# Eight neighbouring rows of an expert's second weights in each partition, and the strided reads that go with them

## What is computed

```python
# E = 8 experts, K = 2 of them for each token, FF = 1024, all float32
router_weights = softmax(xf @ rw + rb);  topw, topi = top_k(router_weights, 2);  topw = softmax(topw)
h   = gelu(einsum('td,edf->etf', xf, w1) + b1[:, None, :], approximate=False)   # w1: (8, 256, 1024)
eo  = einsum('etf,efd->etd', h, w2) + b2[:, None, :]                            # w2: (8, 1024, 256)
out = einsum('etd,te->td', eo, combine)        # combine holds topw at the two chosen experts
```

## Time and profile before

| | us |
|---|---|
| runs shown | 766.80, 769.13, 770.72 |
| median | 769.13 |
| the profiled execution | 768.74 |
| its span (first to last recorded work) | 767.0 |
| TensorE busy in it | 717.6 (94%) |
| DVE / ACT / POOL busy | 498.9 / 370.0 / 287.2 |

### The profile page before, as it was taken

The page is one execution under the profiler, slowest core; times in us unless marked ns, Lnnn a source line. Parts: engine busy times, 40 slices in busy tenths (PEclk is TensorE's granted clock), DMA queues, the critical chain, the costliest instruction groups (busy, mean ns, idle before and its releaser), DMA issues.

```text
span 767.0 us, 14561 instructions
## 1 busy us (share of the span) xinstructions
PE 717.6 (94%) x4969; PEld 482.2 (63%) x4969; DVE 498.9 (65%) x1376; ACT 370.0 (48%) x749; POOL 287.2 (37%) x558
## 2 busy tenths in 40 slices
PE   6889999999999999999988598999999999999983
PEld 4444434535464455555553485898899999999941
DVE  4579788688766877755786443455666666666436
ACT  3325466665757677677743245424333233332403
POOL 8305522543653554535752232312223322322114
PEclk9999999999999999999996799999999999999997
DMA  8954421343253022315037742586999999999754
GB/s 263 287 142 132 116 94 45 84 126 127 51 160 124 13 59 82 91 47 136 16 109 268 238 153 79 184 284 199 332 341 328 334 336 346 335 332 345 236 179 165
DMA packets 95154, 140.29 MB, mean 183 GB/s; under 512 B 11855, under 2 KB 81077, under 8 KB 92597
## 3 DMA queue, kind: packets, MB, share of 16 engines
q1 hardware_dynamic: 76357, 107.86, 44.6%
q10 hardware_dynamic: 15072, 22.02, 8.6%
q0 software_dynamic: 3648, 9.45, 3.5%
HBM read 110.65 MB, written 28.65 MB: 182 GB/s over the span
## 4 chain that ended last, share of the span: by engine, by line
PE 74%; issue 8%; DVE 6%; DMA 6%; POOL 3%; ACT 1%; SPq 0%; DVEq 0%; ACTq 0%; POOLq 0%
PE out_acc L984 12%; PE score_pair L961 10%; PE work L932 9%; PE score_pair L855 8%; PE work L849 8%; PE work L906 6%; PE work L1008 4%; PE score_pair L849 3%; DVE neg_part_max L1469 3%; PE work L855 3%; PE work L918 2%; PE work L992 2%; DMA arena<-parts_scratch 2%; PE work L935 2%; PE out_acc L849 1%
## 5 line engine op out<-in xcount | busy, mean ns | idle before, releaser
L1469 DVE TENSOR_REDUCE neg_part_max<-work 128x1 f32<-128x512 f32 (+4 forms) x368 | 213.1, 624 | 72.5 <-PE work L935 36.0
L1244 ACT ACTIVATE arena<-score_pair 128x1024 f32<-128x1024 f32 (+2 forms) x224 | 179.0, 840 | 74.9 <-PE score_pair L961 73.6
L932 PE MATMUL work<-arena 96*128 96x77 bf16 (+4 forms) x640 | 118.9, 280 | 15.8 <-DMA arena<-parts_scratch 7.8
L961 PE MATMUL score_pair<-arena 99*128 99x512 bf16 (+2 forms) x448 | 104.5, 338 | 2.3 <-DMA arena<-negmax_scratch 1.6
L984 PE MATMUL out_acc<-arena 128*32 128x512 f32 (+4 forms) x896 | 104.6, 521 | 0.8 <-DVE arena L1489 0.8
L1901 POOL DMA_INDIRECT chosen_scratch<-arena,scatter_rows x36 | 35.5, 987 | 177.8 <-DVE arena L1401 177.5
L932 PEld LDWEIGHTS work<-arena 96*128 96x128 bf16 x640 | 50.0, 100 | 79.6 <-issue 35.9
L855 PE MATMUL score_pair<-arena 128*128 128x256 f32 x432 | 97.6, 379 | 0.0
L1957 POOL TENSOR_SCALAR_AFFINE_SELECT arena<-arena 128x256 f32<-128x256 f32 x128 | 51.7, 412 | 117.2 <-ACT arena L1244 116.1
L1177 ACT ACTIVATE arena<-work,expert_b_cols 128x128 f32<-128x128 f32 x180 | 51.2, 370 | 84.1 <-PE work L849 78.3
L849 PE MATMUL work<-arena 128*128 128x128 f32 x720 | 89.1, 282 | 0.3 <-issue 0.3
(11 more groups left out here) (257 smaller groups left out, 958.5 us busy)
## 6 DMA issues: line engine op xcount, KB each, us to landing
arena<-in_L_xattn_e_w SPq DMA_DIRECT2D x54, 1024.0 KB, 5.9
arena<-parts_scratch SPq DMA_DIRECT2D x24, 768.0 KB, 6.2
arena<-in_L_xattn_e_w ACTq DMA_DIRECT2D x18, 1024.0 KB
parts_scratch<-arena_more SPq DMA_DIRECT2D x24, 384.0 KB, 2.6
parts_scratch<-arena_more SPq DMA_DIRECT2D x24, 256.0 KB, 3.0
parts_scratch<-arena_more SPq DMA_DIRECT2D x24, 128.0 KB, 3.0
residual<-in_x SPq DMA_DIRECT2D x4, 512.0 KB, 8.1
tokens_scratch<-residual SPq DMA_DIRECT2D x2, 1024.0 KB, 4.8
```

The costliest lines, as they stand in the source:

```text
L932: m = pe.matmul(bank[:, j * it.w:(j + 1) * it.w], qa[st.half(it.g)][0:R_S, h, n0:n0 + P], k, start=True, stop=not it.last)
L961: m = pe.matmul(st2[pair][0:rows, j, 0:w], k, qa[st.half(it.g)][0:R_M, h, skip:QG], start=True, stop=True)
L1244: act_e.activation(pt[buf][0:rows, :, 0:w], st2[pair][0:rows, :, 0:w], ACT.Exp, scale=float(HD) ** -0.5).then_inc(pair_taken[pair], 1)
L1469: dve.tensor_reduce(pm[:, it.at, it.t, it.h0:it.h0 + it.nh], bank[:, 0:it.nh * it.w].rearrange("p (j k) -> p j k", j=it.nh), AX.X, ALU.max ...
```

## The change

Partition p now holds, for each expert, the hidden units 8p to 8p+7, and block f takes unit 8p + f from each partition. The sum over the hidden units is the same, taken in another order.

- The second weights come as one run of 8 KB to a partition.
- The first weights are loaded as before, but the stationary block f is read as every eighth column (a step of 32 bytes) instead of 128 neighbouring ones.
- The first biases come as eight rows of 4 KB, one for each expert, are turned by eight transposes of 8x128 with every eighth column, and one DVE copy swaps the order of block and expert while it takes them from PSUM.

```diff
-        b1_rows = onat_words[1][0:E * FC, D:D + P]
+        b1_rows = onat_words[1][0:E, D:D + FF].rearrange("e (p f) -> e f p", f=FC)
...
-        w2_view = w2.rearrange("e (c p) n -> p e c n", p=P)
+        w2_view = w2.rearrange("e (p c) n -> p e c n", p=P)
+        w1_columns = [w.rearrange("p c (m f) -> p c f m", f=FC) for w in w1_ring]
...
-                        m = pe.matmul(to[:, q * P:(q + 1) * P], w1_ring[j % RING1][:, c, f * P:(f + 1) * P],
+                        m = pe.matmul(to[:, q * P:(q + 1) * P], w1_columns[j % RING1][:, c, f, :],
                                       slot_xT[j % 2][:, c, :], start=(c == 0), stop=(c == KC - 1))
...
-                    pe.transpose(bank[:, 0:E * FC], b1_rows[:, :], ident[0:E * FC, 0:E * FC]).then_inc(full[it.bank], 1)
+                    for f in range(FC):
+                        m = pe.transpose(bank[:, f * E:(f + 1) * E], b1_rows[:, f, :], ident[0:E, 0:E])
+                    m.then_inc(full[it.bank], 1)
...
-                    dve.tensor_copy(b1_col[:, :], bank[:, 0:E * FC]).then_inc(taken[it.bank], 1)
+                    dve.tensor_copy(b1_col.rearrange("p (e f) -> p e f", e=E), bank[:, 0:E * FC].rearrange(
+                        "p (f e) -> p e f", f=FC)).then_inc(taken[it.bank], 1)
...
-                sp.dma_start(b1_rows[:, :], b1.rearrange("e (c p) -> (e c) p", p=P)).then_inc(b1_in, 16)
+                sp.dma_start(onat_words[1][0:E, D:D + FF], b1).then_inc(b1_in, 16)
```

## The result

The changed kernel took 906.5 us in the median (901.2 to 907.4) against 769.9 for the kernel before beside it: 1.1765 times as long, with a 95% interval of 1.172 to 1.181. The profiled execution took 907.24 us, 138.5 more than the one of before. Rival A went through, a little dearer than its own range, and 11.5 us above the end of the stated one.

What follows compares the result with a forecast made beforehand. It took products alone on TensorE to bound the loop, line 849 paced by weight loads. 768.74 + 0 + 0 + 0.68 = 769.4, plus 0.39 for the runs' median, gives 769.8 us; range 765 to 895.

Steps and rivals of the forecast that it cites:

- Rival A: Strided stationary reads of line 849 take 1.73 to 2 times 111 ns; kernel 860 to 895 us; chance 0.30.
- What bounds the kernel, and what paces line 849: In the expert loop, products alone hold the chain, 7.03 us a tile; line 849 is paced by weight loads, 111 ns.
- Part 1: Every eighth column as stationary block in line 849's 1152 loads: taken to cost 0 us, as DVE's 64-byte step cost nothing.
- The bounds of part 1: For strided weight loads: lower, no cost, from DVE's copy; upper, 1.73 times as long, from GpSimd's 1058 ns against 611.
- Part 2: Second weights in 8 KB runs: some 4% less time for half the weight traffic, off the loop's chain; taken 0 us.
- Part 3: First biases near 217 us: eight transposes for one add 0.68 us on the chain; the DVE copy adds 0.
- Rival B: A strided weight load takes 23 ns more, at DVE's 1.04 ns a place; kernel 797 us; chance 0.07.
- C: 8 KB runs are slower and DMA bounds the loop, 0.9 us a tile more; kernel 793 us; chance 0.05.
- D: Waits before the loop, for a load, a store and a gather, shrink by 5 us; kernel 765 us; chance 0.08.
- Near 6.2 to 7.1 us means A: Line 849's 32 weight loads taking that long on the chain, not 3.57 us, would show Rival A.

## Why the prediction was wrong

- **What bounds the kernel, and what paces line 849: right.** The chain of the loop is products alone, before and after. That the first products are paced by their weight loads and have no slack is what made the loss whole: each nanosecond on a load was to cost 1.15 us, and 123.1 ns x 1.152 is 141.8.
- **Part 1, the choice of 0: wrong, and the step that failed.** It rested on DVE's copy of 512 elements with a 64-byte step, 622 ns, being no longer than contiguous work of that size. The contiguous neighbour was another operation (a tensor_scalar of 353 ns, extended by copies from PSUM). A contiguous copy from SBUF is faster than either, 280 ns for 256 elements, and the strided one lasts 380. The row did hold a penalty, hidden by an unequal comparison. The reason given beside it, that TensorE's read path is like DVE's, rested on no row, and DVE pays too. Of the two nearest rows GpSimd's, copy against a cast, came nearer: 1.73 times, with TensorE's load at 234.7 / 111.6 = 2.10.
- **The bounds of part 1: too low.** GpSimd's 1.73 was taken as the upper end of the cost, and rival A's price stretched it to 2 without a row (its terms add up to 893, put down as 895). The load's 2.10 put the time 11.5 us past the range. The ratio of durations was the wrong measure to carry over: a load's duration grew 335 / 191 = 1.75 times, close to GpSimd's 1.73, but its duration holds some 80 ns (100 when strided: 335 - 235) that overlap with the load before it, and the spacing of the stream, which is what the chain pays, grew 2.10 times. That 1.75 lies so near 1.73 may be chance: no run links the two, and GpSimd's copies of 256 elements grew from 390 to 600 or 630 ns, 1.5 to 1.6 times.
- **The Trainium skill's rule: right on the side that mattered.** The Trainium skill's page SBUF — State Buffer (section "Door 1: The DMA port swizzle") says that at least two reads must fall in one line of 16 bytes for full speed. The runs agree: two elements a line (step 2) cost 118 ns against 110, less than two cost 175, one costs 232. Its other figure, that four float32 is as far as one can step for free, is not what was measured: step 4 costs nearly as much as step 8 (232 and 237 ns for the load, 450 and 461 for the moving operand, 380 and 380 for DVE's copy). I had weighed the rule against one row and let the row decide, where the row did not measure it.
- **Part 2: right.** The long runs alone are 1.0004 times before. The DMA busy share fell by 3% for all traffic at the same rate, where the prediction's 4% on half of it makes 2%, and it was hidden.
- **Part 3: right.** The chain shows the eight transposes at 0.97 us where one took 0.20, 0.77 more against 0.68 forecast. The DVE copy, whose reads in PSUM now step by 32 bytes, took 217 ns against 215:

```profile
217.68 0.97 PE work L1073 x8
```

- **Rival B, C, D.** B's idea, a pace set by places and not by columns, was the right kind of mechanism with the wrong number: it took DVE's 1.04 ns for the price of a line, which is 1.8 for a float32 load. C and D fell with the long runs alone. "Near 6.2 to 7.1 us means A" stood at 7.51.

## What to carry to other kernels

Before a layout makes an operand strided, count the 16-byte lines it touches: for float32, steps of 1 and 2 elements cost little and 3 or more up to double, for a product's stationary and moving operand and for copies on DVE, ACT and GpSimd alike; float32 transposes came no slower, and bf16 products by 10 ns at most. What it costs the kernel depends on what sets the pace of that instruction: beside a moving operand of 256 columns, or at half clock, the same read cost a fifth. And a DMA made cheaper brings nothing while the chain of waits holds no DMA, however full its engines look.

## What was not expected of the hardware

- The price of a line differs by kind: about 1.8 ns for a float32 product's load and moving read; a float32 transpose's load grows from 146 to 188 ns, a bf16 one's from 98 to 148, with 128 lines each, and in the stream the transposes come every 110 ns either way and the bf16 products every 60 to 65 ns for 55. This was measured and not explained.
- Steps of 4 to 16 are not quite equal: loads of 330, 321, 318, 326 and 334 ns for steps 4 to 8, 369 for 12, 312 for 16. No rule was found for this.
- The strided load does not follow TensorE's clock (335 ns at full, 337 at half clock), while one of neighbouring columns goes from 192 to 333 ns.
